# Gated attention block with routed experts: products in alternating PSUM banks, early evictions and O copies divided anew between VectorE and ScalarE

## The chip, the core and the metric

One core of a Trainium2 chip runs the whole program in one launch. The metric is the time of the execution on the device in microseconds. The kernel before takes 844.95 us in the median of three runs (843.52 to 846.76).

## What is computed

The reference, cut to its core (8 batches of 256 channels by 512 positions; 16 heads of 16 channels; 12 experts, two per token):

```python
def _L0_xattn_ref(x, c, Wq, bq, Wk, bk, Wv, bv, Wo, bo):
    q = jnp.einsum('oc,bct->bot', Wq, x) + bq[None, :, None]
    k = jnp.einsum('oc,bct->bot', Wk, c) + bk[None, :, None]
    v = jnp.einsum('oc,bct->bot', Wv, c) + bv[None, :, None]
    ...
    scores = jnp.einsum('bhkt,bhks->bhts', q, k) * SCALE
    p = jax.nn.softmax(scores, axis=-1)
    out = jnp.einsum('bhts,bhks->bhkt', p, v)
    ...
    return jnp.einsum('oc,bct->bot', Wo, out) + bo[None, :, None]
x = x + jnp.tanh(g_xattn[0]) * _L0_xattn_ref(_layernorm(x), ctx_2048, ...)
x = x + jnp.tanh(g_ffn[0]) * _L0_ffn_ref(_layernorm(x), ...)   # top-2 of 12 experts: silu(x w1) * (x w3), then w2
```

## The kernel before

Attention runs as ten slots (`slots`, L352), one after the other. In slot t three batches are at work, each in another part (flags of `slot`): part a makes k, q and v of batch t; part b computes scores, exponentials and the product with V of batch t-1; part c divides batch t-2 by its sums, multiplies it with Wo, adds it to the residual, normalises it and makes the router's logits. Slot 0 has part a only, slot 1 has a and b, slots 2 to 7 have all three, slot 8 has b and c, slot 9 has c only. Slots 2 to 5 are two rounds of a hardware loop. Part p of a slot loads and normalises x and the context of the next batch.

Each slot has 16 steps v. In a step with part b, TensorE makes the scores of step v+1 (four products into the two halves of S0 and S1), then perhaps one "extra" product of part a or c, then the values of step v (matmuls of 32 columns each, L1296, into O; the scores are L1257). ScalarE makes two exponentials of 128x1024 per step (L747). The table `EXTRA` says which extra product belongs to which step: k0, k1, q0, q1 (three passes of fp16 parts, 128x512, L1331), v0 to v3 (128x256, L1313), o0, o1 (the product with Wo, L1331), t0, t1 (transposes of the normed residual, L1347), lg (logits, L1351). There are two PSUM banks for them: MA for all of part a, MC for all of part c. A product of part a waits until the use of MA before it has been evicted (`project`: `wait(pe, g.a_free, t, NA, A_USES[what])`), one of part c likewise for MC (`output`, `g.c_free`). V products use MA's two halves in turn, but with the same wait.

VectorE evicts all of them in its own step v: k and q at L953 (then, after the second half, a cast to fp16 at L960; GpSimd computes the low part, L606, in slot 0 VectorE itself, L874), V at L967, o at L984, t at L987, lg at L989. In the same step order stand: the block of ON_AT = 5 (L938, L941, L874: O times the broadcast inverse sums `zc`, its cast and low part), which is ahead of the eviction of step 5; statistics of x (LN_AT), x normed (XN_AT), the layer norm of part c (XN2_AT, L1009), the cast of the context (CS_AT, L880), the copies of O out of PSUM after steps 3, 7, 11, 15 (L1021), and last the splits of expert weights.

The expert weights (12 experts, 48 quarters) are split into fp16 parts during attention: ScalarE's queue loads a quarter (`load_quarter`, L723) into one of four buffers wf, VectorE splits it (`split_quarter`, L855 and L857) into one of two buffers wp, SyncE stores it (`store_quarter`, L427). The table `quarters(t)` gives the steps. `load_behind` (L726) refills wf and waits for the split (s_wlo); it stands in ScalarE's queue between exponentials, after the exponential of step v+3, and in slot 0 behind all four splits of step 15.

SyncE's queue in a slot, in order: zl (the sums out of osum), zr to `inverse_sums`, four copies over partitions of osum, k's high part to memory (two writes), the broadcast read of zc (L496), k's low part, the loads of the next batch, weight stores of steps 0 to 2, q's high part, K's read back (L474), q's low part, Q's read back, weight stores of steps 3 to 9, the output's store, the store of the normed tokens, the remaining weight stores. Q and K must be back before the first scores of the next slot, which TensorE makes in step 15. In slots 8 and 9 the stores of steps 0 to 8 come before the output's store. In slot 0 filler products (`keep_busy`, L1230) run between the extra products.

After attention come the routing and 43 tiles of experts.

```python
EXTRA = {0: "k0", 1: "k1", 2: "q0", 3: "q1", 4: "v0", 5: "v1", 6: "v2", 8: "o0", 9: "o1",
         10: "v3", 13: "t0", 14: "t1", 15: "lg"}
ON_AT, LN_AT, XN_AT, XN2_AT, CS_AT, SPLIT_AT = 5, 7, 8, 11, 12, 3
```

## Time and profile before

| | |
|---|---|
| median of three runs | 844.95 us (843.52 to 846.76) |
| the profiled execution's own time | 844.76 us |
| its span | 842.9 us |
| granted TensorE clock, mean over the span | 0.861 of full speed |
| TensorE busy / VectorE / ScalarE / GpSimd | 657.0 / 429.9 / 317.6 / 229.0 us |
| moved by DMA | 153.43 MB, mean 182 GB/s |

The span runs from the first instruction to the last of the profiled execution; its own time is what the run's clock gives, 1.9 us more. Busy times are those of instructions; an instruction that waits is not busy. In a row of a timeline, the bracket says how long the engine was idle before it and what ended that. The granted clock is given as a share of 2.4 GHz; its two levels are 1.0 and 0.5.

### The profile page before, as it was taken

How to read it: one execution, taken by the hardware profiler on the slowest of the kernel's cores; microseconds unless marked ns; L12 is line 12 of the kernel's file. 1: busy time of each engine (PE TensorE's matmuls, PEld its weight loads, DVE VectorE, ACT ScalarE, POOL GpSimd, SP SyncE). 2: the span in 40 equal slices, each digit the busy share in tenths (PEclk: the TensorE clock that was granted, in tenths of full speed). 3: DMA queues.
4: the chain of work that ended last, by engine and by line, in shares of the span. 5: the costliest groups of instructions: out<-in, count | busy, mean ns of one | idle time of the engine just before them, and what ended most of it. 6: DMA issues, size and time to landing. Idle time of an engine off the chain costs nothing.

```text
span 842.9 us, 14098 instructions
## 1 busy us (share of the span) xinstructions
PE 657.0 (78%) x4335; PEld 305.1 (36%) x4336; DVE 429.9 (51%) x769; ACT 317.6 (38%) x391; POOL 229.0 (27%) x176
## 2 busy tenths in 40 slices
PE   5728477987797787988898732328999999999993
PEld 4602112232321222323222120225666666666661
DVE  5656455846747567465563845394333333333330
ACT  0014455735565556555577600001222222222221
POOL 4012012411422224122220100143334544354422
PEclk8859869978889988796999865558999999999997
DMA  7576676737738577375576754754776787855433
GB/s 225 178 235 192 205 239 188 258 88 252 245 98 267 157 243 229 87 263 198 164 254 172 213 161 124 246 192 109 194 193 175 198 220 231 217 105 87 87 51 38
DMA packets 64435, 153.43 MB, mean 182 GB/s; under 512 B 8261, under 2 KB 13894, under 8 KB 62854
## 3 DMA queue, kind: packets, MB, share of 16 engines
q1 hardware_dynamic: 44848, 98.58, 35.6%
q0 software_dynamic: 9632, 22.55, 14.0%
q10 hardware_dynamic: 9910, 31.75, 13.0%
q8 instruction: 22, 0.36, 0.2%
q14 instruction: 23, 0.19, 0.1%
HBM read 92.04 MB, written 58.46 MB: 179 GB/s over the span
## 4 chain that ended last, share of the span: by engine, by line
PE 46%; DMA 20%; DVE 16%; issue 9%; POOL 3%; SPq 2%; PEldq 1%; ACT 1%; POOLq 0%; DVEq 0%; ACTq 0%
PE S L1434 15%; PE O L1455 8%; DMA weight_parts<-wp 6%; DMA ocz<-inverse_sums 6%; PE O L1296 6%; PE MA L1331 4%; DMA out<-yo,slot_out 3%; PE MC L1351 3%; PE S L1257 3%; DMA q_parts<-qs 3%; DVE wp L857 2%; PE MC L1331 2%; PE S L1421 2%; DVE wp L855 2%; POOL rstd L612 1%
## 5 line engine op out<-in xcount | busy, mean ns | idle before, releaser
L747 ACT ACTIVATE prob<-S 128x1024 f32<-128x1024 f32 x256 | 245.7, 1023 | 229.3 <-PE S L1257 158.4
L1296 PE MATMUL O<-prob,V 128*32 128x512 f32 x1024 | 155.0, 681 | 0.0
L1434 PE MATMUL S<-W,xT 128*128 x1032 | 149.0, 301 | 1.2 <-DVE xT L1197 1.2
L1257 PE MATMUL S<-Q,K 48*128 48x512 f16 x512 | 92.9, 422 | 51.6 <-ACT prob L747 43.7
L1434 PEld LDWEIGHTS S<-W,xT 128*128 128x128 f16 x1032 | 99.9, 98 | 38.5 <-issue 1.4
L676 POOL DMA_INDIRECT out<-yo,slot_out x43 | 68.9, 1603 | 121.6 <-ACT yo L797 71.4
L1455 PE MATMUL O<-W,hT 128*128 (+1 forms) x344 | 90.3, 381 | 1.0 <-DVE hT L1217 1.0
L1257 PEld LDWEIGHTS S<-Q,K 48*128 48x128 f16 x512 | 19.8, 95 | 180.4 <-ACT prob L747 150.8
L1205 DVE SCALAR_TENSOR_TENSOR hh<-S,act 128x320 f32<-128x320 f32 x43 | 21.1, 492 | 122.1 <-PE S L1434 122.1
L857 DVE SCALAR_TENSOR_TENSOR wp<-wf,wp 128x1024 f16<-128x1024 f32 x48 | 73.2, 1526 | 1.7
L610 POOL TENSOR_SCALAR veps<-mv 128x2 f32<-128x2 f32 x16 | 6.2, 385 | 197.7 <-DVE mv L997 101.6
L855 DVE TENSOR_SCALAR wp<-wf 128x1024 f16<-128x1024 f32 x48 | 37.8, 787 | 38.1 <-DMA weight_parts<-wp 37.8
L652 POOL DMA_INDIRECT xg<-tokens_normed,slot_tok x43 | 42.4, 987 | 42.6 <-PE S L1421 30.1
L1313 PE MATMUL MA<-w4s,cs 128*128 128x256 f16 x192 | 29.5, 295 | 29.7 <-DVE V L967 27.5
L797 ACT ACTIVATE yo<-O,slot_w 128x512 f32<-128x512 f32 x43 | 29.6, 687 | 60.3 <-PE O L1455 56.2
L606 POOL TENSOR_TENSOR ks<-kf,ks 128x1024 f16<-128x1024 f32 x7 | 15.3, 2190 | 130.3 <-DVE ks L960 130.3
L1455 PEld LDWEIGHTS O<-W,hT 128*128 128x128 f16 (+1 forms) x344 | 31.6, 97 | 49.4 <-issue 29.1
L791 ACT ACTIVATE hs<-hh 128x320 f16<-128x320 f32 x43 | 20.2, 470 | 77.6 <-DVE hh L1205 77.6
L784 ACT ACTIVATE act<-S 128x320 f32<-128x320 f32 x43 | 18.8, 437 | 79.7 <-PE S L1434 72.8
L1217 DVE COPY hT<-S 128x640 f16<-128x640 f16 x43 | 21.1, 491 | 41.4 <-PE S L1445 41.4
L1296 PEld LDWEIGHTS O<-prob,V 128*32 128x32 f32 x1024 | 21.1, 113 | 46.6 <-issue 34.2
L1331 PE MATMUL MC<-os,w4s 128*128 128x512 f16 x96 | 27.3, 427 | 13.6 <-DVE os L941 10.7
(152 smaller groups left out, 706.2 us busy)
## 6 DMA issues: line engine op xcount, KB each, us to landing
wf<-wall ACTq DMA_DIRECT2D x48, 512.0 KB, 5.7
weight_parts<-wp SPq DMA_DIRECT2D x46, 512.0 KB, 6.9
W<-weight_parts SPq DMA_DIRECT2D x10, 2048.0 KB, 10.3
K<-k_parts SPq DMA_DIRECT2D x8, 1024.0 KB, 9.7
Q<-q_parts SPq DMA_DIRECT2D x8, 1024.0 KB, 7.4
k_parts<-ks SPq DMA_DIRECT2D x24, 256.0 KB
q_parts<-qs SPq DMA_DIRECT2D x24, 256.0 KB
ctx<-ctx_in SPq DMA_DIRECT2D x8, 512.0 KB, 10.4
```

Of the source, the lines that this page charges most:

```text
L652: pool.indirect_dma_start(out=xg[j % TR][:, :], out_offset=None, in_=xn_dram[:, :], in_offset=bass.IndirectOffsetOnAxis(ap=slot_tok[:, j:j ...
L676: pool.indirect_dma_start(out=out[:, :], out_offset=bass.IndirectOffsetOnAxis(ap=slot_out[:, j:j + 1], axis=0), in_=yo[j % TR][:, :], in_o ...
L747: act.activation(prob[:, u % RING, :], S[u % 2][:, :], ACT.Exp, scale=SCALE).then_inc(g.exp, 1)
L797: act.activation(yo[n % TR][:, :], y_ps[:, :], ACT.Copy, scale=slot_w[:, bass.ds(j.value(), 1)])\
L855: dve.tensor_scalar(c[:, 0], w[:, :], WS, None, ALU.mult).then_inc(s_whi, 1)
L857: dve.scalar_tensor_tensor(out=c[:, 1], in0=w[:, :], scalar=WS, in1=c[:, 0], op0=ALU.mult, op1=ALU.subtract).then_inc(s_wlo, 1)
L1257: last = pe.matmul(S[u % 2][:, s * T:(s + 1) * T], K[par][r0:r0 + rows_, 2 * g4 + n, st * P:(st + 1) * P], Q[par][r0:r0 + rows_, 2 * g4 + ...
L1296: last = pe.matmul(O[g4 % 2][2 * DK * j:2 * DK * (j + 1), :], V[par][:, st, head(g4, j), :], prob[:, u % RING, (j % 2) * T:(j % 2 + 1) * T ...
L1313: last = pe.matmul(MA[:, i * C:(i + 1) * C], cs[:, xp, k, m * P:(m + 1) * P], w4s[:, wp_, 2, k, :], start=(n == 0 and k == 0), stop=(n == ...
L1331: last = pe.matmul(bank[:, :], w4s[:, wp_, w, k, m * P:(m + 1) * P], src[:, xp, k, :], start=(n == 0), stop=(n == 3 * CT - 1))
L1434: last = pe.matmul(ps, xT[par][:, xp * TT + k, :], W[:, bass.ds(off + (w * WCOL + (2 * k + n) * F), F)], start=(k == 0 and (xp, w) == (0, 0)),
L1455: last = pe.matmul(y_ps[:, :], hT[par][0:rows_, block, :], W[0:rows_, bass.ds(off + (w * WCOL + W2 + k * T), T)], start=(n == 0), stop=(n ...
```

## The change

The extra products of parts a and c now stand in one list, ORDER, and take MA and MC in turn, so that consecutive products never share a bank; each waits for the eviction of the product before last, k0 of the next slot for all of part a and the last logits. v3 moves from step 10 to 7, t0 and t1 from 13 and 14 to 12 and 13. On VectorE the eviction of a step of part a now comes ahead of the block of step 5; the statistics of x move from step 7 to 6, the cast of the context from 12 to 10. ScalarE evicts k and q in slot 0, and in all slots copies O out of PSUM after the groups 0, 1 and 2 (behind the exponentials 11, 19 and 27); VectorE keeps the copy of group 3. The weight quarters are spread otherwise: none in slot 0 (four before), eight in slot 1, four in slots 2 to 7 at steps 2, 7, 12, 14 (2, 6, 9, 12 before), ten in slot 8 (eight before), four in slot 9 at steps 2, 2, 10, 10 (two at 7 before). On SyncE the read of zc goes ahead of k's writes, q's low part ahead of K's read, and in slot 0 the loads of the next batch go first. GpSimd makes its constants in slot 0 only after x's low part.

```diff
+        ORDER = ("k0", "k1", "q0", "q1", "v0", "v1", "v2", "v3", "o0", "o1", "t0", "t1", "lg")
+        EXTRA = {0: "k0", 1: "k1", 2: "q0", 3: "q1", 4: "v0", 5: "v1", 6: "v2", 7: "v3", 8: "o0", 9: "o1",
+                 12: "t0", 13: "t1", 15: "lg"}
+        ON_AT, LN_AT, XN_AT, CS_AT, XN2_AT, SPLIT_AT = 5, 6, 8, 10, 11, 3
+        def bank(name):
+            return (MA, MC)[ORDER.index(name) % 2]
-        BUSY = {"k0": 4, "k1": 10, "q0": 4, "q1": 8, "v0": 3, "v1": 3, "v2": 3, "v3": 8}
+        BUSY = {"k1": 14, "q1": 6, "v0": 2, "v1": 2, "v2": 2, "v3": 6}
...
             if t.i is None and t.add == 0:
-                steps, first = (15, 15, 15, 15), At(None, 0, 0)
-            elif t.i is None and t.add == 1:
-                steps, first = (1, 3, 5, 7, 9, 11, 13, 14), At(None, 0, 4)
+                return []
+            first = At(t.i, 4 * t.mul, 4 * t.add)
+            if t.i is None and t.add == 1:
+                steps, first = (1, 3, 5, 7, 9, 11, 13, 14), At(None, 0, 0)
             elif t.i is None and t.add == B:
-                steps, first = (0, 2, 4, 6, 8, 10, 12, 13), At(None, 0, QUARTERS - 12)
+                steps = (0, 2, 4, 6, 7, 9, 10, 11, 12, 13)
             elif t.i is None and t.add == B + 1:
-                steps, first = (7, 7), At(None, 0, QUARTERS - 4)
+                steps, first = (2, 2, 10, 10), At(None, 0, QUARTERS - 6)
             else:
-                steps, first = (2, 6, 9, 12), At(t.i, 4 * t.mul, 4 * t.add + 4)
+                steps = (2, 7, 12, 14)
...
+                            for name in ("k0", "k1", "q0", "q1"):
+                                m = int(name[1])
+                                f, bias = (qf, bq_c) if name[0] == "q" else (kf, bk_c)
+                                act.wait_ge(g.a_full, A_USES[name] + 1)
+                                act.activation(f[:, m, :], bank(name)[:, :], ACT.Identity, scale=1.0 / WS,
+                                               bias=bias[:, m:m + 1]).then_inc(g.a_free, 1)
...
+                        if u % (2 * TT) == 2 * TT - 1 + 4 - 2 * TT and u > 2 * TT:
+                            g4 = u // (2 * TT) - 1
+                            wait(act, g.pv, b, VS, TT * (g4 + 1))
+                            wait(act, g.oz, b, OZ, 16 - OZ)
+                            act.activation(osum[1 - par][:, g4 % 2 * CT + g4 // 2, :], O[g4 % 2][:, :], ACT.Copy)\
+                                .then_inc(g.os, 1)
...
-                    wait(pe, g.a_free, t, NA, A_USES[what])
+                    n = A_USES[what]
+                    if n == 0:
+                        wait(pe, g.a_free, t, NA)
+                        wait(pe, g.c_free, t, NCU, 1 - 2 * NCU)
+                    elif n >= 2:
+                        wait(pe, g.a_free, t, NA, n - 1)
+                    into = bank(what)
...
+                def output(b, name, a):
+                    into, n = bank(name), C_USES[name]
+                    if a and n < 2:
+                        wait(pe, g.a_free, b, NA, 3 * NA + n - 1)
+                    wait(pe, g.c_free, b, NCU, 1 + {"o0": 0, "o1": 0, "t0": 1, "t1": 2, "lg": 4}[name])
...
+                            pool.wait_ge(g.xl, 1)
                             constants()
```

Three places in the order of the instructions. The first is VectorE in slot 2, from the eviction of v0 (step 4) on; `wp` is a weight split, `osum<-O` a copy out of O, `f_oz` the arrival of zc. Before:

```order
L967 SCALAR_TENSOR_TENSOR V<-MA,bv_all 128x16x16 [waits f_pv,f_a_full]
...
L938 TENSOR_TENSOR kf<-osum,ocz 128x1024 [waits f_kl]
L941 CAST os<-kf 128x1024 [waits f_on]
L874 TENSOR_TENSOR os<-kf,os 128x1024 [waits f_oh]
...
L967 SCALAR_TENSOR_TENSOR V<-MA,bv_all 128x16x16 [waits f_a_full]
...
L967 SCALAR_TENSOR_TENSOR V<-MA,bv_all 128x16x16 [waits f_a_full]
L855 TENSOR_SCALAR wp<-wf 128x1024 [waits s_tanh,s_wst1,s_wf1]
...
L857 SCALAR_TENSOR_TENSOR wp<-wf,wp 128x1024 [waits s_whi]
```

and now:

```order
L982 SCALAR_TENSOR_TENSOR V<-MA,bv_all 128x16x16 [waits f_pv,f_a_full]
...
L982 SCALAR_TENSOR_TENSOR V<-MC,bv_all 128x16x16 [waits f_a_full]
...
L995 TENSOR_TENSOR kf<-osum,ocz 128x1024 [waits f_kl]
L998 CAST os<-kf 128x1024 [waits f_on]
L902 TENSOR_TENSOR os<-kf,os 128x1024 [waits f_oh]
...
L982 SCALAR_TENSOR_TENSOR V<-MA,bv_all 128x16x16 [waits f_a_full]
...
L916 BN_AGGR mv<-stats 128x2 [waits f_bst,s_tanh]
...
L982 SCALAR_TENSOR_TENSOR V<-MC,bv_all 128x16x16 [waits f_a_full]
L883 TENSOR_SCALAR wp<-wf 128x1024 [waits s_tanh,s_wst1,s_wf1]
...
L885 SCALAR_TENSOR_TENSOR wp<-wf,wp 128x1024 [waits s_whi]
```

The block that waits for zc (L938 before, L995 now) has moved behind the eviction of v1; the copy of O is gone; the split comes after v3's eviction instead of v2's.

The second is ScalarE at the start, from the warming exponential to the first real ones (`prob`). Before:

```order
L719 ACTIVATE warm_exp<-ones 128x1
L723 DMA wf<-wall 128x1024 x4
L723 DMA wf<-wall 128x1024 [waits s_wlo] x4
L747 ACTIVATE prob<-S 128x1024 [waits f_full] x4
```

and now:

```order
L730 ACTIVATE warm_exp<-ones 128x1
L734 DMA wf<-wall 128x1024 x2
L756 ACTIVATE kf<-MA,cols 128x512 [waits f_a_full,s_wq]
L756 ACTIVATE kf<-MC,cols 128x512 [waits f_a_full]
L756 ACTIVATE qf<-MA,cols 128x512 [waits f_a_full]
L756 ACTIVATE qf<-MC,cols 128x512 [waits f_a_full]
L734 DMA wf<-wall 128x1024 x2
L769 ACTIVATE prob<-S 128x1024 [waits f_full] x4
L769 ACTIVATE prob<-S 128x1024 [waits f_pv,f_full] x6
L734 DMA wf<-wall 128x1024 [waits s_wlo]
L769 ACTIVATE prob<-S 128x1024 [waits f_pv,f_full] x2
L774 ACTIVATE osum<-O 128x512 [waits f_pv]
```

The four weight loads that wait for splits (s_wlo) are gone from ahead of the first exponential; four evictions out of MA and MC stand there, and a copy of O stands behind the twelfth exponential.

The third is SyncE in slot 2, from k's first write to the first weight store behind Q's read. Before:

```order
L471 DMA k_parts<-ks 8x16x1024 [waits f_kh]
L471 DMA k_parts<-ks 8x16x1024
...
L496 DMA ocz<-inverse_sums 128x1x1024 [waits f_zst]
L471 DMA k_parts<-ks 8x16x1024 [waits f_kl]
...
L427 DMA weight_parts<-wp 256x1x1024
L471 DMA q_parts<-qs 8x16x1024 [waits f_qh,s_bog]
L471 DMA q_parts<-qs 8x16x1024
...
L474 DMA K<-k_parts 128x4x1024 [waits f_full]
L471 DMA q_parts<-qs 8x16x1024 [waits f_ql,s_bog]
L474 DMA Q<-q_parts 128x4x1024 [waits f_qst,s_bog]
...
L427 DMA weight_parts<-wp 256x1x1024
```

and now:

```order
L507 DMA ocz<-inverse_sums 128x1x1024 [waits f_zst]
...
L477 DMA k_parts<-ks 8x16x1024 [waits f_kh]
L477 DMA k_parts<-ks 8x16x1024
L477 DMA k_parts<-ks 8x16x1024 [waits f_kl,s_bog]
...
L433 DMA weight_parts<-wp 256x1x1024
L477 DMA q_parts<-qs 8x16x1024 [waits f_qh,s_bog]
L477 DMA q_parts<-qs 8x16x1024
L477 DMA q_parts<-qs 8x16x1024 [waits f_ql,s_bog]
...
L480 DMA K<-k_parts 128x4x1024 [waits f_full]
L480 DMA Q<-q_parts 128x4x1024 [waits f_qst,s_bog]
...
L433 DMA weight_parts<-wp 256x1x1024
```

The read of zc (`ocz<-inverse_sums`) has gone ahead of k's writes, q's third write ahead of K's read, and one weight store has gone from behind Q's read.

## Rows read from the trace of the kernel before

**Rows 1.** Windows: stretch, us, busy PE, PEld, DVE, ACT, POOL, clock, DMA, GB/s.
```profile
0.00:58.57 58.57, 28.97 (x174) 22.59 (x175) 35.86 (x51) 1.58 (x3) 14.78 (x26) 0.77 0.64 203
58.57:120.11 61.54, 40.35 (x240) 9.57 (x240) 31.94 (x39) 30.57 (x33) 10.21 (x6) 0.81 0.67 214
120.11:395.97 275.86, 230.16 (x1372) 73.03 (x1372) 167.91 (x249) 154.09 (x160) 71.52 (x45) 0.85 0.65 203
395.97:445.28 49.31, 43.55 (x278) 12.87 (x276) 28.14 (x42) 30.88 (x32) 8.65 (x5) 0.92 0.63 192
445.28:499.90 54.62, 37.50 (x234) 10.94 (x232) 30.30 (x42) 30.20 (x32) 3.06 (x3) 0.87 0.68 196
499.90:535.80 35.90, 11.81 (x38) 6.88 (x38) 18.00 (x69) 0.00 (x0) 3.05 (x3) 0.55 0.48 150
```

**Rows 2.** Timeline, slot 0: start us, us, engine, line, what, [idle before <- releaser].
```profile
17.32 0.74 DVE L953 TENSOR_SCALAR kf<-MA,cols 128x512 f32<-128x512 f32 x1
...
28.23 0.69 DVE L960 CAST qs<-qf 128x1024 f16<-128x1024 f32 x1
...
28.95 1.23 DVE L874 TENSOR_TENSOR qs<-qf,qs 128x1024 f16<-128x1024 f32 x1
...
31.77 0.57 SPq L471 DMA_DIRECT2D q_parts<-qs  x1
...
40.40 0.36 SPq L474 DMA_DIRECT2D Q<-q_parts  x1
...
45.94 1.03 PE L1257 MATMUL S<-Q,K 48*128 48x512 f16 x4 [6.28 <-DMA Q<-q_parts]
...
58.57 1.94 ACT L747 ACTIVATE prob<-S 128x1024 f32<-128x1024 f32 x2 [46.62 <-DVE wp L857]
```

**Rows 3.** Timeline of TensorE, slot 3 (176.93 to 233.50 us).
```profile
183.56 0.61 PE L1257 MATMUL S<-Q,K 48*128 48x512 f16 x4
184.10 1.47 PE L1331 MATMUL MA<-cs,w4s 128*128 128x512 f16 x6
185.50 1.06 PE L1296 MATMUL O<-prob,V 128*32 128x512 f32 x8
...
202.02 1.46 PE L1313 MATMUL MA<-w4s,cs 128*128 128x256 f16 x6 [4.46 <-DVE V L967]
...
226.53 0.92 PE L1347 MATMUL MC<-ident,xn 128*128 128x128 f32 x4 [3.73 <-DVE xT L987]
```

**Rows 4.** Timeline of slot 7.
```profile
420.42 0.83 PE L1313 MATMUL MA<-w4s,cs 128*128 128x256 f16 x6 [4.06 <-DVE V L967]
...
441.38 0.65 PE L1347 MATMUL MC<-ident,xn 128*128 128x128 f32 x4 [1.07 <-DVE xT L987]
...
442.96 1.96 PE L1351 MATMUL MC<-gate,xT 128*128 128x12 f32 x16
```

**Rows 5.** Timeline of VectorE, slot 3.
```profile
198.42 1.22 DVE L938 TENSOR_TENSOR kf<-osum,ocz 128x1024 f32<-128x1024 f32 x1 [4.23 <-DMA ocz<-inverse_sums]
```

**Rows 6.** Timeline of SyncE's DMA issues, slot 3.
```profile
211.09 0.37 SPq L474 DMA_DIRECT2D Q<-q_parts  x1
```

**Rows 7.** Timeline of VectorE, slot 1.
```profile
100.67 0.69 DVE L855 TENSOR_SCALAR wp<-wf 128x1024 f16<-128x1024 f32 x1 [12.17 <-DMA weight_parts<-wp]
```

**Rows 8.** Timeline of slot 8.
```profile
465.03 0.69 DVE L855 TENSOR_SCALAR wp<-wf 128x1024 f16<-128x1024 f32 x1 [10.03 <-DMA weight_parts<-wp]
...
491.09 0.69 DVE L855 TENSOR_SCALAR wp<-wf 128x1024 f16<-128x1024 f32 x1 [3.68 <-DMA weight_parts<-wp]
```

**Rows 9.** Timeline of slot 9.
```profile
520.54 2.74 PE L1331 MATMUL MC<-os,w4s 128*128 128x512 f16 x6 [2.84 <-DVE residual L984]
```

**Rows 10.** The page's part 6: issues, KB each, median us to landing.
```profile
weight_parts<-wp SPq DMA_DIRECT2D x46, 512.0 KB, 6.9
...
Q<-q_parts SPq DMA_DIRECT2D x8, 1024.0 KB, 7.4
```

**Rows 11.** The page's part 5: a 128x512 copy on ScalarE.
```profile
L797 ACT ACTIVATE yo<-O,slot_w 128x512 f32<-128x512 f32 x43 | 29.6, 687 | 60.3 <-PE O L1455 56.2
```

More of the change, by code:

```diff
@@ L741, in slot @@
                         return
+                    if not guard and t.i is None and t.add == 1:
+                        for n in range(2, WFS):
+                            load_quarter(At(None, 0, n))
                     b = t.before(1)
@@ L1317, in project, with three @@
                         w, src, hi, lo = (1, xs, g.xh, g.xl) if what[0] == "q" else (0, cs, g.ch, g.cl)
[L1318 removed]
+                        last = three(into, w, m, src, t, hi, lo, m == 0, 1)
                     last.then_inc(g.a_full, 1)
[L1321 to L1323 removed]
+                def three(into, w, m, src, b, hi, lo, first, c):
+                    for n in range(3 * CT):
                         (wp_, xp), k = PASSES[n // CT], n % CT
```

120 lines of the change are left out of this document (57 added, 63 removed).

## The prediction

> **What bounds the kernel now.** I read the windows first, cut at the first exponential of each slot [rows 1]. Attention takes 535.8 of the 842.9 us: slot 0 58.57, slot 1 61.54, slots 2 to 6 together 275.86 (55.2 each), slot 7 49.31, slot 8 54.62, slot 9 35.90. What follows (routing, experts) is 307.1 us; the change edits nothing in it. In slots 2 to 6 TensorE is busy 46.0 us of 55.2 at a granted clock of 0.85, VectorE 33.6, ScalarE 30.8, the DMA share is 0.65: no engine is full, so waits and the low clock are what can be won.
>
> The timelines say which waits. Slot 0: the scores can start at 45.94, once Q has landed, yet the first exponential comes at 58.57, after 46.62 us idle that a weight split of VectorE (L857) ended [rows 2]: ScalarE's queue stood at a weight load that needs a split of step 15. Slot 3: a V product stands 4.46 us for the eviction of the one before it, and the second transpose group 3.73 us [rows 3]. The cause of the first is that VectorE had the block of step 5 ahead of that eviction, and the block waited 4.23 us for the broadcast inverse sums [rows 5]. After each such stop the products run at half pace, 1.46 us for what takes 0.83 elsewhere [rows 3, 4]: the granted clock fell from 2.4 to 1.2 GHz while TensorE stood. Slot 7 has the same two stops, 4.06 and 1.07 us [rows 4].
>
> **Slot 0.** Two things go. First, the split wait: 58.57 less 45.94 and the 0.6 us of the first score pair is 12.0 us. Second, the path to Q. Before, k0 is evicted at 17.32 on VectorE, behind all of its work on x, and k1, q0, q1 follow one by one through one bank; the low part of q ends at 30.2 (28.95 + 1.23), its write is issued at 31.77, Q's read at 40.40 [rows 2]. After, ScalarE evicts, so VectorE only does cast and subtraction for k and for q behind its x work: from about 17.3 (or 1.7 earlier, since the V memsets of GpSimd no longer stand beside it) 2 x (0.69 + 1.23) = 3.8 us, to 21, and 0.5 us of waits: 21.5, 8.7 us earlier. The write of q's low part also no longer stands behind K's read, which I put at 0.9. So the first exponential moves by 12.0 + 8.7 + 0.9 = **21.6 us**, to 37.0. Bounds: 11.6 (the low clock and the earlier loads of batch 1 eat the path's gain) and 25.
>
> **Slot 1.** It has no output part; eight products and eight splits. Its large loss is VectorE standing 12.17 us for the store of a weight quarter [rows 7], because SyncE held that store behind the write of q, K's read and Q's. Now the second store goes ahead of K's read, but stores three to five still follow Q's. I count Q's read issued some 25 us into the slot, the third store 1 us later, 6.9 us each [rows 10]: step 9's split is possible at 33, then one store and one split (6.9 + 1.9 = 8.8 us, less overlap over two buffers) to the split of step 14 at 45.5. So 47.0, **14.5 less**; bounds 42 and 56.
>
> **Slots 2 to 6.** With every product in time, at the upper clock, a step with a 512-wide three-pass product takes 0.61 + 1.47 + 1.06 less 0.2 of overlap = 2.94 us [rows 3]; there are six (k0, k1, q0, q1, o0, o1): 17.6. Four V steps: 0.61 + 0.83 + 1.06 - 0.2 = 2.3, so 9.2. Two transpose steps with 0.65 instead: 2.2, so 4.4 [rows 4]. The logits: 0.61 + 1.96 + 1.06 - 0.1 = 3.5 [rows 4]. Three bare steps at ScalarE's two exponentials, 30.8/16 = 1.93 each [rows 1], 5.8. Sum 40.5. ScalarE's three copies cost 3 x 0.69 of its time [rows 11]; the one beside o1 is covered by that step's 2.94, the two beside v1 and t1 stick out by 2 x 0.97 + 0.69 - 2.3 = 0.3 each: 41.1. What waits remain? The block of step 5 now follows v1's eviction, and v2 and v3 need only v0's and v1's, so the broadcast can land at 17 us without stopping TensorE; behind it stand v2's eviction, one split and o0, so o0 is late next. At the end of the slot VectorE has the layer norm, t0, a split, t1, a split and lg's eviction nearly back to back, and the next k0, now in lg's bank, waits for that last one; ScalarE's fourth weight load waits for the split of step 14. I add 3.9 us for these two together: **45.0** a slot, 10.2 less, 50.9 in all. The nearest check is slot 7: 49.31 less its two stops (4.06 + 1.07) is 44.2, with part of the slow clock still in it. Bounds: 41.5 (no waits) and 50. Q's read was issued 34 us into slot 3 (211.09) and takes 7.4 us [rows 6, 10]: landing at 41.6 even if nothing of that chain gets shorter, just when the next slot's scores ask for it.
>
> **Slot 7**: 44.2, less the slow stretch behind the stops, plus 0.6 for the copies: 43.5, **5.8 less** (bounds 42 and 47).
>
> **Slot 8 gets longer.** It takes ten quarters for eight, since slot 0 takes none. Today VectorE stands 10.03 us for a store near the start and 3.68 us at the last quarter [rows 8]. The first wait stays (same place, same zc read before the store). The two extra splits are 2 x 1.92 = 3.8 us. SyncE stores quarters of steps up to 8 at once; those of 9 to 13 stand behind the store of the normed tokens, which needs the layer norm of step 11. So the split of step 11 (same buffer as step 9's) waits for that whole chain, and the one of step 13 for step 11's store, 6.9 us [rows 10]; today one quarter waits so. I take 4.7 us for the second wait, less 3 x 0.69 = 2.1 for the copies that VectorE loses: **+6.4**, to 61.0; bounds 0 and +12.
>
> **Slot 9**: two splits (3.8 us) now sit between o1's statistics and the layer norm, of which 1.1 cover the wait for rstd; zl's read stands behind the last store, about 2; but o1 no longer waits for o0's eviction, 2.84 [rows 9], nor t1 for t0's (0.8). Together **+1.1**. The experts' first weights wait for those stores; their reads end some 20 us before use, so that is free.
>
> **Sum.** -21.6 - 14.5 - 50.9 - 5.8 + 6.4 + 1.1 = -85.3 against the profiled execution's own 844.76 us (span 842.9): 759.5, say **760**. The median of the runs shown is 844.95, the same to 0.2. The bounds of all terms at once give 724 and 815; half of that spread either way is 742 to 783.
>
> A rule against the change is weighed here. In rows, TensorE at the upper clock is what a short idle in every step (about 0.4 us between pairs of exponentials) still leaves in slot 7, 0.92 in the mean [rows 1]. The Trainium skill, "TensorE: Matmul & The Clock Gate", section "A second HAM failure mode: psum-queue depth-cycling", says that a kernel whose product groups cycle through banks idles TensorE briefly between groups and so flips between the clock's levels. By that rule alternating MA and MC would win no clock.
>
> **Rivals.**
> A. *The clock does not recover* (what the skill's rule would give). TensorE keeps 46.0 us of work per slot as now, plus 3 us idle: 49 in slots 2 to 6, +20, and slot 7 at 47, +3.5: about 784. For it: 0.81 to 0.85 in every slot with loads. Against it: 0.92 in slot 7, whose stops were shorter. 0.10.
> B. *DMA becomes the bound.* 55.2 us at a share of 0.65 is 36 us of transfer; in 45 us that is 0.80, and bursts will stretch Q's read by some 5 us or more, beyond the 41.6 above. Slots of 50: +25 and slot 7 +3: 788. 0.10.
> C. *The waits only move*: each slot still ends with VectorE (o0 late, then t0, lg), and only the start is won: -21.6 - 14.5 + 7.5 and 2 us a slot: 804. 0.06.
> D. *Slower.* ScalarE's queue is the mechanism: a weight load stands in it and waits for a split, and the split for a store (as at 58.57 and in slot 1). If the later steps (7, 12, 14) put such a stop of 12.17 us [rows 7] into each of slots 1 to 8, the whole gain is given back, 8 x 12.2 = 97: 857. It decides from 10.7 us a slot on. Against it: in slot 3 there is room between Q's read at 34 us and step 14 for two stores. 0.03.
> That the edit does not do what it says (bank waits kept by the semaphores' counts) is unlikely: the listing has v1's and v3's products in MC, with waits for the use before last. It would look like C.
>
> **How the numbers follow.** My forecast 0.70, A 0.10, B 0.10, C 0.06, D 0.03, 0.01 below all. The range holds the forecast's own 742 to 783 and A and B: 742 to 796. Faster by over 0.5% (about what a measurement here tells from no change) 0.95, within 0.5% 0.02, slower 0.03.
>
> **What would show it.** First exponential near 37 us, four activations from MA and MC ahead of it; slots 2 to 6 at 43 to 47 with the clock above 0.92; no V product waiting for V; no Q wait over 1 us at a slot's end; slot 8 near 61 with a DMA wait before the split of step 11. I am wrong if slots 2 to 6 stay above 50, or if ScalarE stands for a split at their ends.

## The result, and the profile after

The changed kernel takes 779.5 us (median of 4 runs, 776.3 to 780.2) against 845.1 (843.5 to 846.8): a ratio of 0.9216, 95% interval 0.9186 to 0.9247. The forecast was 760, its range 742 to 796. The profiled execution has a span of 778.4 us, 64.5 less than before. Of executions over 1.5% above the fastest of their kernel, one is e7's (839.4 us), one e11's (763.2) and three are e9's (the profiled one among them); they are in the medians and not in the ratios below.

The windows, cut at the same events as before (the first exponential of each slot; for slot 9 the last addition's start and the end of the logits' copy), show where they went. Columns as in [rows 1].

```profile
0.00:38.53 38.53, 26.33 (x152) 21.50 (x153) 19.90 (x39) 4.33 (x7) 13.35 (x26) 0.91 0.76 246
38.53:96.44 57.91, 43.40 (x242) 9.72 (x240) 30.39 (x36) 32.00 (x36) 10.59 (x6) 0.79 0.65 209
96.44:328.54 232.10, 215.67 (x1372) 69.92 (x1372) 157.25 (x234) 161.29 (x175) 67.98 (x45) 0.91 0.72 233
328.54:370.17 41.63, 41.00 (x278) 12.69 (x276) 25.14 (x39) 32.25 (x36) 7.34 (x5) 0.96 0.72 235
370.17:429.40 59.23, 39.94 (x234) 11.22 (x232) 30.53 (x43) 31.70 (x35) 4.38 (x3) 0.84 0.67 214
429.40:464.64 35.24, 11.10 (x38) 7.17 (x38) 21.75 (x73) 0.00 (x0) 4.45 (x3) 0.55 0.49 149
464.64:778.40 313.76, 264.58 (x2003) 169.08 (x2003) 117.92 (x281) 70.27 (x132) 117.21 (x88) 0.91 0.62 160
```

| stretch | before, us | after, us | difference | forecast |
|---|---|---|---|---|
| slot 0 | 58.57 | 38.53 | -20.0 | -21.6 |
| slot 1 | 61.54 | 57.91 | -3.6 | -14.5 |
| slots 2 to 6, each | 55.2 | 46.4 | -43.8 in all | -50.9 in all |
| slot 7 | 49.31 | 41.63 | -7.7 | -5.8 |
| slot 8 | 54.62 | 59.23 | +4.6 | +6.4 |
| slot 9 | 34.98 | 35.24 | +0.3 | +1.1 |
| routing and experts | 308.02 | 313.76 | +5.7 | 0 |

(In [rows 1] slot 9 was ended 0.9 us later; the last two rows of the table use the end of the logits' copy in both.)

**Slot 0**, the timeline: VectorE's low part of q, the read of Q, the first scores, the first exponential.

```profile
20.82 1.23 DVE L902 TENSOR_TENSOR qs<-qf,qs 128x1024 f16<-128x1024 f32 x1
32.52 0.36 SPq L480 DMA_DIRECT2D Q<-q_parts  x1
37.88 1.04 PE L1286 MATMUL S<-Q,K 48*128 48x512 f16 x4 [7.59 <-DMA Q<-q_parts]
38.53 3.77 ACT L769 ACTIVATE prob<-S 128x1024 f32<-128x1024 f32 x4 [18.57 <-PE S L1286]
```

Against [rows 2] the scores start 8.1 us earlier (37.88 for 45.94) and ScalarE no longer stands for a split, which is the other 12.0.

**A steady slot** (slot 4, 188.44 to 235.01). First TensorE (a V product, the first transposes, the logits), then VectorE, GpSimd, and two of SyncE's issues.

```profile
205.65 0.83 PE L1347 MATMUL MC<-w4s,cs 128*128 128x256 f16 x6
...
224.06 0.66 PE L1382 MATMUL MA<-ident,xn 128*128 128x128 f32 x4 [1.39 <-DVE xn L1037]
...
231.68 2.66 PE L1386 MATMUL MA<-gate,xT 128*128 128x12 f32 x16 [2.15 <-DVE xT L1015]
```
```profile
206.86 1.22 DVE L995 TENSOR_TENSOR kf<-osum,ocz 128x1024 f32<-128x1024 f32 x1
...
213.57 1.29 DVE L913 BATCH_NORM_STATS2 stats<-residual 128x6 f32 x2 [3.17 <-DMA residual<-x]
...
225.70 2.25 DVE L883 TENSOR_SCALAR wp<-wf 128x1024 f16<-128x1024 f32 x1
227.99 3.04 DVE L885 SCALAR_TENSOR_TENSOR wp<-wf,wp 128x1024 f16<-128x1024 f32 x1
230.95 0.68 DVE L1015 COPY xT<-MC 128x512 f32<-128x512 f32 x1
```
```profile
225.27 2.14 POOL L639 TENSOR_TENSOR xs<-xn,xs 128x1024 f16<-128x1024 f32 x1 [1.85 <-DVE xs L1040]
227.36 2.58 POOL L616 TENSOR_TENSOR cs<-ctx,cs 128x1024 f16<-128x1024 f32 x1
```
```profile
197.65 0.65 SPq L507 DMA_DIRECT2D ocz<-inverse_sums  x1
...
218.52 0.36 SPq L480 DMA_DIRECT2D Q<-q_parts  x1
```

The V product runs in 0.83 us with no wait, where one stood 4.46 before [rows 3]. The block of step 5 no longer waits for the broadcast sums in any of slots 2 to 7 (4.23 before in slot 3, [rows 5], and 3.5 to 4.7 in the others): SyncE issued their read 9.2 us into the slot. Before, it was 11.7 us into slot 3, behind the two writes of k's high part:

```profile
188.65 0.63 SPq L496 DMA_DIRECT2D ocz<-inverse_sums  x1
```

What is left on TensorE are two short waits. The second has a readable cause: the split of step 12 takes 5.29 us here instead of its usual 1.91, because both of its halves run beside an operation of GpSimd, and t1's eviction (230.95) stands behind it, and the logits (231.68) behind that.

**Slot 1**: three of the five splits that waited on VectorE, SyncE's issues, and two windows of it.

```profile
64.79 0.69 DVE L883 TENSOR_SCALAR wp<-wf 128x1024 f16<-128x1024 f32 x1 [5.65 <-DMA weight_parts<-wp]
70.81 0.69 DVE L883 TENSOR_SCALAR wp<-wf 128x1024 f16<-128x1024 f32 x1 [2.01 <-DMA weight_parts<-wp]
80.71 0.69 DVE L883 TENSOR_SCALAR wp<-wf 128x1024 f16<-128x1024 f32 x1 [6.31 <-DMA weight_parts<-wp]
```
```profile
58.51 0.58 SPq L433 DMA_DIRECT2D weight_parts<-wp  x1
59.13 0.62 SPq L480 DMA_DIRECT2D K<-k_parts  x1
69.63 0.37 SPq L480 DMA_DIRECT2D Q<-q_parts  x1
70.05 26.30 SPq L433 DMA_DIRECT2D weight_parts<-wp  x6
```
```profile
60.00:70.00 10.00, 6.16 (x47) 1.74 (x50) 3.97 (x8) 5.97 (x8) 0.93 (x2) 0.94 0.96 327
70.00:80.00 10.00, 9.72 (x44) 1.08 (x36) 3.53 (x5) 5.27 (x6) 2.13 (x1) 0.54 0.91 314
```

Q's read goes out 31.1 us into the slot, and the third store behind it. The store of 58.51 lets its buffer go at 70.8, 12.3 us later, that of 70.05 at 80.7, 10.7 us later, with the DMA share at 0.96 and 0.91. VectorE's five waits come to 18.9 us (the three shown, and 1.88 and 3.06). Before, beside the 12.17 us of [rows 7] and one of 0.33, there were two more of slot 1:

```profile
84.23 0.69 DVE L855 TENSOR_SCALAR wp<-wf 128x1024 f16<-128x1024 f32 x1 [1.51 <-DMA weight_parts<-wp]
115.22 0.69 DVE L855 TENSOR_SCALAR wp<-wf 128x1024 f16<-128x1024 f32 x1 [3.90 <-DMA weight_parts<-wp]
```

That is 17.9 us, so the long wait is gone and the time spent in waits is not. ScalarE, whose weight loads wait for these splits, stood 16.9 us in slot 1 before and 18.0 now.

**Slot 8**: VectorE's three longest waits for a store; the first is that of [rows 8], the second is new.

```profile
390.39 0.69 DVE L883 TENSOR_SCALAR wp<-wf 128x1024 f16<-128x1024 f32 x1 [9.97 <-DMA weight_parts<-wp]
418.13 0.69 DVE L883 TENSOR_SCALAR wp<-wf 128x1024 f16<-128x1024 f32 x1 [7.04 <-DMA weight_parts<-wp]
426.56 0.69 DVE L883 TENSOR_SCALAR wp<-wf 128x1024 f16<-128x1024 f32 x1 [3.42 <-DMA weight_parts<-wp]
```

**Routing**: ScalarE's queue, then VectorE.

```profile
467.63 10.36 ACTq L414 DMA_DIRECT2D W<-weight_parts  x2
478.03 0.22 ACT L798 ACTIVATE el<-dl 128x16 f32<-128x16 f32 x1 [55.26 <-DMA W<-weight_parts]
```
```profile
478.28 0.17 DVE L1112 TENSOR_SCALAR el<-el 128x16 f32<-128x16 f32 x1 [5.90 <-ACT el L798]
```

The first expert's load is issued at 467.63, after the last stores; the second waits for the first's landing, and the Exp of the routing weights stands behind it in ScalarE's queue. Before, the loads were issued from 523.03 on, the first 20 us ahead of the Exp, which then waited for nothing but its operand:

```profile
543.10 0.21 ACT L770 ACTIVATE el<-dl 128x16 f32<-128x16 f32 x1 [56.10 <-DVE dl L1071]
```

### The profile page after: what moved, and what is told of

It is laid out like the page before. It is cut to its first block, busy times and chain, and to the rows that moved or that the text cites. A ratio compares the mean times of both kernels' runs of the same rounds, so it can differ in the third digit from the quotient of the medians.

```text
span 778.4 us, 14056 instructions
## 1 busy us (share of the span) xinstructions
PE 642.0 (82%) x4313; PEld 301.3 (39%) x4314; DVE 402.9 (52%) x741; ACT 331.8 (43%) x419; POOL 225.3 (29%) x176
## 4 chain that ended last, share of the span: by engine, by line
PE 45%; DMA 25%; DVE 12%; issue 8%; POOL 5%; SPq 3%; ACT 1%; POOLq 0%; DVEq 0%; ACTq 0%
PE S L1468 16%; PE O L1489 9%; DMA weight_parts<-wp 9%; DMA residual<-x 5%; PE O L1325 4%; DMA out<-yo,slot_out 4%; PE MA L1365 3%; DMA q_parts<-qs 3%; PE MA L1386 3%; PE S L1286 3%; DVE wp L883 2%; PE S L1455 2%; PE MC L1365 2%; DVE wp L885 2%; DMA zl<-osum 1%
## 5 line engine op out<-in xcount | busy, mean ns | idle before, releaser
L1325 PE MATMUL O<-prob,V 128*32 128x512 f32 x1024 | 148.7, 655 | 0.0
L883 DVE TENSOR_SCALAR wp<-wf 128x1024 f16<-128x1024 f32 x48 | 41.2, 859 | 42.1 <-DMA weight_parts<-wp 42.0
L1246 DVE COPY hT<-S 128x640 f16<-128x640 f16 x43 | 21.2, 492 | 41.1 <-PE S L1479 41.1
L1386 PE MATMUL MA<-gate,xT 128*128 128x12 f32 x128 | 24.4, 333 | 17.2 <-DVE xT L1015 17.2
L1325 PEld LDWEIGHTS O<-prob,V 128*32 128x32 f32 x1024 | 20.8, 112 | 45.0 <-issue 32.1
L1386 PEld LDWEIGHTS MA<-gate,xT 128*128 128x128 f32 x128 | 23.6, 284 | 23.9 <-DVE xT L1015 23.1
```

The source lines that it names most:

```text
L883: dve.tensor_scalar(c[:, 0], w[:, :], WS, None, ALU.mult).then_inc(s_whi, 1)
L1325: last = pe.matmul(O[g4 % 2][2 * DK * j:2 * DK * (j + 1), :], V[par][:, st, head(g4, j), :], prob[:, u % RING, (j % 2) * T:(j % 2 + 1) * T ...
L1386: last = pe.matmul(into[:, m * NE:(m + 1) * NE], xT2[:, m, k * P:(k + 1) * P], gate[:, k, :], start=(k == 0), stop=(k == TT - 1))
```

## The experiments

The theory after this first look was that of the prediction: alternating banks and evictions ahead of the block took the steady slot's stops away. Its rival: the stops went because what the block waited for now comes in time, by SyncE's order or by the table of steps.

In the table a slot is the mean of slots 2 to 6 in the trace (first exponential to first exponential); before it was 55.2. Each job timed the kernel before beside its own (843.6 to 846.1 us), and the ratio is to that. One trace was kept of each kernel; the change and two kernels that differ from it only elsewhere (e8, e12) give slots of 46.4 to 46.6, so differences of a few tenths of a microsecond in this column mean nothing.

| run | median, us | ratio, interval | slot, us |
|---|---|---|---|
| the change | 779.5 | 0.9216 [0.9186, 0.9247] | 46.4 |
| e1 one bank per kind | 778.1 | 0.9229 [0.9170, 0.9288] | 45.4 |
| e2 block first | 778.0 | 0.9219 [0.9168, 0.9270] | 45.1 |
| e3 both | 780.9 | 0.9226 [0.9172, 0.9279] | 45.7 |
| e4 copies on VectorE | 779.3 | 0.9212 [0.9164, 0.9260] | 46.7 |
| e5 SyncE's old order | 783.5 | 0.9289 [0.9220, 0.9358] | 47.7 |
| e6 = e3 and e5 | 806.2 | 0.9575 [0.9536, 0.9615] | 49.8 |
| e7 kernel before, new SyncE order | 826.2 | 0.9802 [0.9753, 0.9851] | 51.7 |
| e8 Exp ahead of the load | 774.2 | 0.9189 [0.9137, 0.9241] | 46.6 |
| e9 = e3 and the old places | 811.0 (793.9 to 813.8) | none, see there | 51.3 |
| e10 = e8 and other places | 762.7 | 0.9050 [0.9007, 0.9094] | 43.5 |
| e11 = e10, two quarters in slot 0 | 755.7 | 0.8928 [0.8861, 0.8995] | 43.8 |
| e12 slot 0 evicted by VectorE | 776.2 | 0.9195 [0.9168, 0.9223] | 46.5 |

**e1, one bank per kind of product again.**

```
 def bank(name):
-    return (MA, MC)[ORDER.index(name) % 2]
+    return MA if name in A_USES else MC
...
+                    wait(pe, g.a_free, t, NA, A_USES[what])
```

> The changed kernel with one part undone: part a's products all go to MA again and part c's to MC, each waiting for the eviction before it. The order of VectorE's work, ScalarE's share, the weight table and SyncE's order stay new. My theory: most of the gain of slots 2 to 6 came from moving evictions ahead of the block that waits for zc, so one bank per part costs only what is left: o1 waits for o0's eviction, which comes 2.5 us after o1's product starts now, and slot 0 loses about 1.5 us; some 3 us a slot, 795 to 800 us. Rival: the alternating banks are the whole gain of these slots, then 820 us or more. Second rival: banks are worth nothing, 780 us.

**e2, the block of step 5 ahead of the eviction again** (the `if c and v == ON_AT:` part stands before `if a and name in A_USES:`).

> The changed kernel with the block of step 5 (the one that waits for zc) put back ahead of the eviction of v1; banks alternate as in the change. My theory: v2 needs only v0's eviction and v3 has 4 us of room, so 0 to 1 us a slot: 780 to 786 us. Rival: the order is the whole gain and the banks none: 820 us.

**e3, both at once.**

> Both of them undone together in the changed kernel. Then v2 waits for v1's eviction behind the block again (4.5 us and about 2 us of half pace behind it, per slot, six slots, plus the 3 us of the first run): my theory 815 to 825 us. If the two were independent, the two single losses would add up, to some 800 us.

**e4, ScalarE's three copies out of O back on VectorE.**

```
-                        if u % (2 * TT) == 2 * TT - 1 + 4 - 2 * TT and u > 2 * TT:
-                            act.activation(osum[1 - par][:, ...], O[g4 % 2][:, :], ACT.Copy)
...
-                            if g4 == GROUPS - 1:
+                            wait(dve, g.pv, bb, VS, v + 1)
+                            dve.tensor_copy(osum[1 - par][:, at, :], O[g4 % 2][:, :])
```

> The changed kernel with all four copies out of O on VectorE, as before. My theory: VectorE is what ends the slots now (the eviction of t1 behind a split, then the logits), so 0.69 us more ahead of t0 costs 1 to 2 us a slot in slots 2 to 6, less elsewhere: 785 to 792 us. Rival: ScalarE's 0.6 us copies are on the path of the exponentials, then it gets faster by up to 0.7 us a slot: 774 us.

All four measure like the change itself: 778.0 to 780.9 us, every interval over the others, slots of 45.1 to 46.7. The theories behind e1, e3 and e4 are refuted (795 to 800, 815 to 825 and 785 to 792 us), e2 came 2 us under its 780 to 786, and of the rivals e1's second, "banks are worth nothing, 780 us", is the one that holds. The two things that the change is named after, and the copies, are worth nothing that this measurement can tell as long as the rest of the change is there. In e3 VectorE's block shows why: in slot 4 it starts without a wait, though it stands ahead of the eviction in one bank. Over slots 2 to 7 it waits in two (0.31 and 0.88 us), and TensorE's V product behind it 1.1 us a slot.

```profile
210.70 2.21 DVE L965 TENSOR_TENSOR kf<-osum,ocz 128x1024 f32<-128x1024 f32 x1
```

So the theory fell in this form, and a new one was set up: SyncE's read of the inverse sums, now ahead of the write of k's high part, is what lets the block start in time.

**e5, SyncE's old order in the slots with all three parts; e6, the same on top of e3.**

```
                     if a and c:
+                        wait(sp, g.kh, t, 1, 1)
+                        write(k_dram, ks, 0, (0, 1), g.kst)
                     if c:
                         wait(sp, g.zst, bc, 16, 16)
                         sp.dma_start(zc..., z_dram...)
...
-                        write(q_dram, qs, 1, (1,), g.qst)
                         read(K, k_dram)
+                        write(q_dram, qs, 1, (1,), g.qst)
```

> SyncE's order of the kernel before put back in the slots that hold all three parts (k's high part written ahead of the read of zc, q's low part behind K's read), everything else as in the changed kernel. Theory S (after the first four runs): the stop at the attention output's block in slots 2 to 6 was VectorE waiting for zc, which SyncE issued only behind k's high part; the block now stands behind the same slot's eviction, so VectorE's stop comes back but the next products of TensorE have already been released by the eviction ahead of it: a small loss, 780 to 795 us. Rival (the order on SyncE is worth nothing either): within 0.5% of 778. If SyncE's order alone carries the gain: 810 to 830 us.

> One bank per kind and the block ahead of the eviction, as in the run that undid both, and SyncE's old order with it. Theory S: with neither the early read of zc nor the protection of banks and eviction order, the stop that the kernel before shows in every steady slot (VectorE's block 4.2 us, TensorE's waits 4.1 and 1.1 us in slot 7, a slot of 55.3 us against 46.4) comes back: about 5 slots by 6 to 9 us more, 810 to 825 us. Rival (the table of steps or the copies made by ScalarE carry the gain): within 0.5% of 780.

e5 measures 783.5, inside the new theory's 780 to 795, though its interval still overlaps the change's; e6 measures 806.2, 4 below the theory's 810 to 825 and 26 above its rival's 780. In e5 VectorE's block waits again (the row of VectorE, slot 4):

```profile
213.75 1.23 DVE L1004 TENSOR_TENSOR kf<-osum,ocz 128x1024 f32<-128x1024 f32 x1 [1.65 <-DMA ocz<-inverse_sums]
```

and TensorE has no stop there, since the eviction came first. In e6 the same lateness reaches TensorE; the V product of slot 4 is [rows 3] come back:

```profile
219.78 1.46 PE L1351 MATMUL MA<-w4s,cs 128*128 128x256 f16 x6 [4.08 <-DVE V L1004]
```
```profile
216.18 1.23 DVE L974 TENSOR_TENSOR kf<-osum,ocz 128x1024 f32<-128x1024 f32 x1 [3.86 <-DMA ocz<-inverse_sums]
```

Either cure is enough: SyncE's new order, or the banks with the eviction ahead. Together they give no more than the measurement can tell from one of them. The two edits put back more than the read of the sums (q's low part goes behind K's read, and a weight store behind Q's), so a run with the read alone was needed.

**e7, the kernel before with SyncE's read of the sums ahead of k's write, and nothing else.**

```
-                    if a:
-                        wait(sp, g.qk, t, KQ_READS, 0, s_bog)
-                        wait(sp, g.kh, t, 1, 1)
-                        write(k_dram, ks, 0, (0, 1), g.kst)
                     if c:
                         wait(sp, g.zst, bc, 16, 16)
                         sp.dma_start(zc..., z_dram...)
                     if a:
+                        wait(sp, g.qk, t, KQ_READS, 0, s_bog)
+                        wait(sp, g.kh, t, 1, 1)
+                        write(k_dram, ks, 0, (0, 1), g.kst)
```

> The kernel before with one thing changed: SyncE reads zc before it writes k's high part, in all slots that hold both. Theory S: the early zc removes the stop at the block by itself, so slots 2 to 7 fall from 55.3 towards 47 us: 790 to 805 us. Rival T (table of steps, copies by VectorE at the end of a group, and late evictions also hold the slot): 825 to 840 us. Rival U: no change, 845 us.

826.2 us (824.7 to 839.4): 17.4 of the 65 us come from moving the read of the sums ahead of k's first two writes. That is rival T's outcome, not theory S's (790 to 805). The V product's stop has shrunk to 1.14 us a slot, and the other one of [rows 3], the second transposes, has grown from 3.73 to 5.46 us (TensorE, then VectorE, slot 5):

```profile
322.72 1.11 PE L1345 MATMUL MC<-ident,xn 128*128 128x128 f32 x4 [5.46 <-DVE xT L985]
```
```profile
314.34 2.24 DVE L878 CAST cs<-ctx 128x1024 f16<-128x1024 f32 x1
320.04 0.69 DVE L853 TENSOR_SCALAR wp<-wf 128x1024 f16<-128x1024 f32 x1 [3.46 <-DMA weight_parts<-wp]
```

t0's eviction stands at step 13 behind the cast of the context and the split of step 12, and that split waits 3.46 us for a store. In the change t0's product is at step 12 and its eviction ahead of that split, so the places (the table of steps) looked like the third part.

**e9, the old places in e3**: v3 at 10, t0 at 13, t1 at 14, statistics at 7, the context's cast at 12, splits at 2, 6, 9, 12.

```
-                 12: "t0", 13: "t1", 15: "lg"}
-        ON_AT, LN_AT, XN_AT, CS_AT, XN2_AT, SPLIT_AT = 5, 6, 8, 10, 11, 3
+                 10: "v3", 13: "t0", 14: "t1", 15: "lg"}
+        ON_AT, LN_AT, XN_AT, XN2_AT, CS_AT, SPLIT_AT = 5, 7, 8, 11, 12, 3
...
-                steps = (2, 7, 12, 14)
+                steps = (2, 6, 9, 12)
```

> One bank per kind and the block ahead of the eviction, as in the run that undid both (780.9 us, a steady slot of 46 us), and with it the table of steps of the kernel before: v3 at step 10, t0 and t1 at 13 and 14, the norm's statistics at 7, the cast of the context at 12, splits at 2, 6, 9 and 12. SyncE's new order and ScalarE's copies stay. Theory P (places): the kernel before with SyncE's new order alone still stopped 5.5 us a slot, at its product t1 waiting for t0's eviction behind the split and the cast of step 12 (51.3 us a slot); with the old places that stop comes back: 5 us in each of six or seven slots, 800 to 815 us. Rival: ScalarE's copies are what shortened the slot in the end, and the places are worth nothing: within 0.7% of 781 us.

Its four executions took 793.9 to 813.8 us, so no ratio with an interval stands here. Each is slower than e3's slowest (785.9) and outside the rival's 0.7% about 781 us, so the places are worth something; how much is open. The 793.9, the one whose granted clock (0.90) is that of e3's executions, is 13 us above e3's median: 2 a slot, and below theory P's 800 to 815. The trace is of an execution of 812.9 us, and its slot of 51.3 us holds the lower clock too (0.87 in slots 2 to 6 for e3's 0.93). The stop that theory P named is in it, as in e7, 3.09 us in slot 4 (3.1 to 4.0 in slots 2 to 6):

```profile
243.59 1.11 PE L1374 MATMUL MC<-ident,xn 128*128 128x128 f32 x4 [3.09 <-DVE xT L1015]
```

The account of a steady slot, in us: before 55.2; the early read of the sums alone 51.7 (e7); with the new places and the rest of the change but banks and eviction order 45.7 (e3); with these too 46.4 (the change). The early read is worth 3.5, and from the other side, e6 to e3, SyncE's whole order 4.1. Of the 6.0 between e7 and e3 the copies carry nothing that e4 shows, and the places some 2 by the one execution above; how the other 4 divide between the places and what else differs (SyncE's other moves, ScalarE's share, the clock) is not shown.

**e8, the Exp ahead of the second expert's load.**

```
-            for e in range(EB // 2):
-                if e >= 1:
-                    act.wait_ge(s_wr, 16 * PIECES * e)
-                load_expert(act, e)
+            load_expert(act, 0)
             act.wait_ge(s_wexp, 1)
             act.activation(el[:, :], dl[:, :], ACT.Exp).then_inc(s_wexp, 1)
             act.activation(warm[:, :], ones[:, 0:1], ACT.Silu)
+            for e in range(1, EB // 2):
+                act.wait_ge(s_wr, 16 * PIECES * e)
+                load_expert(act, e)
```

> The changed kernel with ScalarE's Exp of the routing weights issued ahead of the wait for the first expert's landing, that is ahead of the second expert's load instead of behind it. Theory: the 5.9 us that VectorE waits at 478.28 us for this Exp leave the routing stage, and the second expert's load isn't late for its first user: 772 to 775 us. Rival: the routing's other inputs or the expert weights end the stage at the same time, and nothing moves: 778 us.

774.2 us (770.3 to 776.8), inside the theory's 772 to 775. That is 5.4 below the change's median, but 2.3 by the ratios, whose intervals overlap; the trace decides. In it the stretch from the logits' copy to the end takes 306.2 us for 313.8 in the change and 308.0 before; in every other trace with the change's order of Exp and load it takes 312 to 315. ScalarE and VectorE, the routing:

```profile
470.25 0.22 ACT L792 ACTIVATE el<-dl 128x16 f32<-128x16 f32 x1 [48.21 <-DVE dl L1097]
```
```profile
471.29 0.17 DVE L1109 TENSOR_SCALAR el<-el 128x16 f32<-128x16 f32 x1
```

The Exp follows its operand, and VectorE goes on at once.

**e10, e8 with the splits of a steady slot elsewhere.**

```
-                steps = (2, 7, 12, 14)
+                steps = (2, 6, 13, 14)
-        ON_AT, LN_AT, XN_AT, CS_AT, XN2_AT, SPLIT_AT = 5, 6, 8, 10, 11, 3
+        ON_AT, LN_AT, XN_AT, CS_AT, XN2_AT, SPLIT_AT = 5, 7, 8, 10, 11, 3
```

> The changed kernel with the Exp ahead of the second expert's load (774.15 us) and the four splits of a steady slot at steps 2, 6, 13 and 14 instead of 2, 7, 12 and 14, the norm's statistics at step 7 instead of 6. Theory: the split of step 12 stands beside two operations of GpSimd, takes 5.3 us instead of 1.9, and holds back t1's eviction, for which TensorE waits 2.1 us; the split of step 7 can run in the 3.2 us in which VectorE waits for x. Slots 2 to 6 fall by 1 to 3 us each: 760 to 769 us. Rival: the slot is bound by TensorE's own work and ScalarE's exponentials (46.4 us with 43.1 busy), and the waits are made up: 774 us. Against it: the fourth split may end later and stop ScalarE at its load, or the store of step 6 may be late for step 14: up to 780 us.

762.7 us, 11.5 below e8 and inside the theory's 760 to 769. Slots 2 to 6 as one window, then a row of TensorE and two of VectorE in slot 4:

```profile
94.50:311.90 217.40, 204.92 (x1380) 64.57 (x1380) 148.06 (x235) 160.82 (x176) 64.04 (x45) 0.97 0.75 245
```
```profile
183.52 0.54 PE L1283 MATMUL S<-Q,K 48*128 48x512 f16 x2 [2.40 <-ACT prob L769]
```
```profile
205.40 1.22 DVE L882 SCALAR_TENSOR_TENSOR wp<-wf,wp 128x1024 f16<-128x1024 f32 x1
206.88 1.27 DVE L910 BATCH_NORM_STATS2 stats<-residual 128x6 f32 x2
```

A split fills the time in which VectorE stood for x, and no product of TensorE waits for an eviction; the granted clock is 0.97, and a slot 43.5 us. What remains is TensorE's wait for ScalarE at the slot's start (2.40 us here, 5.71 in slot 2, under 1.0 in the three others); in slot 4 ScalarE's queue then holds a weight load that waits for the split of step 14.

**e11, e10 with two of the 48 quarters split at the end of slot 0**, and eight instead of ten in slot 8. The two weight loads that refill their buffers stand behind the exponentials 3 and 5 of slot 1.

```
-                return []
-            first = At(t.i, 4 * t.mul, 4 * t.add)
+                return [(15, At(None, 0, 0)), (15, At(None, 0, 1))]
+            first = At(t.i, 4 * t.mul, 4 * t.add + 2)
...
-                steps = (0, 2, 4, 6, 7, 9, 10, 11, 12, 13)
+                steps = (0, 2, 4, 6, 8, 10, 12, 13)
```

> As the run with the splits at 2, 6, 13 and 14, and two of the quarters are split at the end of slot 0 instead of in slot 8, whose ten become eight (slot 1 keeps eight). Theory: slot 8 takes 59.2 us because its splits wait for stores of the weights (TensorE's longest waits there are 9.97 and 7.04 us), about 5 us less with two fewer; slot 1 gets two more stores ahead of its own and may lose up to 2 us: 3 to 5 us below the run without. Rival: slot 1 loses as much as slot 8 gains: the same time.

755.7 us, 7.0 below e10 and more than the 3 to 5 expected; the fastest kernel here, 88.5 below its own job's 844.2 (its slowest run, 763.2, lies among e10's, the intervals of the ratios do not meet). Slot 8 went from 60.2 to 52.3 us, and slot 1 did not get longer (56.1 for 55.8). VectorE in slot 8 keeps the first wait and one of the last two:

```profile
375.28 0.69 DVE L883 TENSOR_SCALAR wp<-wf 128x1024 f16<-128x1024 f32 x1 [10.61 <-DMA weight_parts<-wp]
403.57 0.69 DVE L883 TENSOR_SCALAR wp<-wf 128x1024 f16<-128x1024 f32 x1 [6.06 <-DMA weight_parts<-wp]
```

**e12, the change with slot 0's four evictions on VectorE.**

```
-                            for name in ("k0", "k1", "q0", "q1"):
-                                act.wait_ge(g.a_full, A_USES[name] + 1)
-                                act.activation(f[:, m, :], bank(name)[:, :], ACT.Identity, ...)
...
-                                if b_:
-                                    dve.tensor_scalar(f[:, m, :], bank(name)[:, :], ...)
+                                dve.tensor_scalar(f[:, m, :], bank(name)[:, :], ...)
```

> The changed kernel with k0, k1, q0 and q1 of slot 0 evicted by VectorE again instead of ScalarE; banks, splits and SyncE's order as changed. In the changed kernel slot 0 is 20 us shorter than before: 12 us of that is the wait for the splits, which this kernel leaves out too, and 8 us is the earlier landing of Q. Theory: VectorE's four evictions of 0.75 us and the waits for them in its queue put the low part of q back from 22.05 by some 3 of those 8 us, the rest of the 8 being the alternating banks, the order on SyncE and GpSimd's later memsets: first exponential at 41 to 43, time 780 to 784 us. Rival (ScalarE is what gained the 8 us): first exponential near 46, 785 to 788 us. Rival 2 (the DMA landing of K and Q is the bound, whoever evicts): 38.5, 779 us.

776.2 us (775.9 to 780.9), the same as the change, where the theory had 780 to 784. VectorE ends q's low part at 23.85 instead of 22.05, and the scores start 1.0 us later:

```profile
22.62 1.23 DVE L895 TENSOR_TENSOR qs<-qf,qs 128x1024 f16<-128x1024 f32 x1
```
```profile
38.88 1.03 PE L1278 MATMUL S<-Q,K 48*128 48x512 f16 x4 [7.13 <-DMA Q<-q_parts]
```

So rival 2 was nearest. Even the 1.0 us is hardly more than chance: e2, e4, e5, e8 and e10 have the change's slot 0, and their scores start anywhere from 37.43 to 38.61. e1, e3, e6 and e9 have one bank per kind there; q's low part ends at 24.1 to 27.2 and the scores start at 37.3 to 41.3, so the alternating banks are worth between nothing and some 3 us. Of slot 0's 20 us, 12.0 are the splits that left, and ScalarE's evictions are 1.0 at most. The rest of the 8 (the next batch's loads issued first, q's low part ahead of K's read, GpSimd's memsets later: VectorE's normalization took 2.74 us beside them and takes 1.00 now) was not tried one by one.

## Why the prediction was right or wrong, point by point

The sign, the range and the two largest terms held; the sum of -85.3 was 20.8 us too large (slot 1 makes 10.9 of that, slots 2 to 6 7.1 and the routing 5.7, while slots 0, 7, 8 and 9 together take 2.9 back), and the reason given for the largest term was not the one that the runs show.

- **Slot 0**, -21.6 against -20.0: right in size, 12.0 as worked out and 8.1 for 9.6. But most of the 8.1 was put down to ScalarE's evictions, and e12 shows them worth 1.0 at most. Q's read stands behind K's in SyncE's queue and waits until q's writes have landed. That q's low part and the scores both came 8.1 us earlier is no proof that one moved the other: in the kernels whose low part ends between 20.6 and 24.5 us the scores start between 37.2 and 38.9, in no order.
- **Slot 1**, -14.5 against -3.6: the mis-sized term. The mechanism (stores behind Q's read, two buffers) is the one in the trace; two sizes were off. Q's read was put at 25 us into the slot and went out at 31.1, which is 6.1 of the 10.9 us. A store was taken at 6.9 us, the median of the whole kernel, and the third took 10.7, which is 3.8 more. By its own bounds (42 to 56) the slot at 57.9 lies outside. No run changes slot 1 alone, so this is read from the trace and not tested; in the other kernels with the change's order there it takes 55.4 to 58.7 us.
- **Slots 2 to 6**, 45.0 against 46.4, right to 3%. "The block of step 5 now follows v1's eviction, so the broadcast can land at 17 us without stopping TensorE" is true and not needed: e1 to e3 undo it and lose nothing, since SyncE's reordering, which the prediction did not price for these slots, already brings the broadcast in time (e5, e6, e7). The second stop of [rows 3] is back wherever the old places are (e7, e9), which the prediction did not price either. For what stays late it added 3.9 us, and the slot has 5.3 over its 41.1. Of the places that it named, the split between t0 and t1 is the one that shows: it costs 5.29 us and not 1.92 beside GpSimd, and the logits wait for t1's eviction behind it. In slot 4 neither o0 nor the next k0 waits. e10 moves the split and gets 43.5, inside the bounds of 41.5 and 50.
- **Slot 7**, -5.8 against -7.7, and **slot 8**, +6.4 against +4.6: right in kind. The second long wait (7.04 us for the 4.7 added) is where it was put, before the split of step 11; e11 shows the price of the two extra quarters, 7.9 us of that slot. **Slot 9**: +0.3 for +1.1.
- **Routing**, 0 against +5.7: the step "the experts' first weights wait for those stores; their reads end some 20 us before use, so that is free" failed. It asked who uses the weights, not what stands behind their load on the issuing engine: the Exp, and VectorE behind it. In e8 that wait of 5.90 us is gone and the stretch is 306.2 us long, below the 308.0 before.
- **Rivals.** A and the clock: the granted clock rose from 0.85 to 0.91 in slots 2 to 6, where the forecast's test was above 0.92, and the slots came out at 46.4 for A's 49. It is 0.97 in e10, whose products wait for no eviction, and 0.90 in e6 and 0.85 before, with stops of some 4 us in every slot; but e7, with the longest single stops (4.9 to 7.2 us), has 0.90, so their length alone does not order it. Nor does the number of banks: 0.95 and 0.93 with one per kind (e1, e3), 0.95 and 0.91 with two (e2, the change). The Trainium skill, "TensorE: Matmul & The Clock Gate", section "A second HAM failure mode: psum-queue depth-cycling", says that in a kernel that cycles through banks TensorE idles briefly between groups of products, often enough for the clock to go back and forth; here cycling cost nothing that the times show, and the measurement decides. B: the share rose to 0.72, no wait for Q appears at a steady slot's end, but in slot 1 the share stood at 0.96 and 0.91 for 20 us, which B had not looked at. C and D did not come about as totals. D's mechanism, ScalarE's queue behind a split, is there: four stops of 18.0 us together in slot 1 and three of 12.7 in slot 8, none in slots 2 to 7.
- **The range.** By the prediction's own terms, all lower bounds at once give 726 us (it has 724) and all upper ones 813 (it has 815), and half of the upper spread ends at 786, not 783. The measured 779.5 lies inside the 742 to 783 all the same, though the misses in slot 1, the steady slots and the routing nearly used it up.
